# Visit tables, GAT weight preparation and first node stage as one block of a two-layer graph network kernel

## The reference, cut to what matters

```
h = relu(layernorm(x))                      # x: 6250 x 256
x = x + layer0(h, src, dst)                 # GAT attention (4 heads), then q/k attention
h = relu(layernorm(x))
x = x + layer1(h, src, dst, edge_type, edge_weight)   # typed GAT (8 heads), layernorm, FFN
# GAT of layer 0, the first that reads the node table:
hw = h @ gat_W;  a_src, a_dst = sums of hw * att_src, hw * att_dst per head
alpha = segment_softmax(leaky_relu(a_src[src] + a_dst[dst]), dst)
x1 = segment_sum(hw[src] * alpha, dst)
```

## Time and profile before

| | |
|---|---|
| median of 3 runs | 4923.0 us (4912.32 to 4923.89) |
| profiled execution, its own time | 4959.05 us |
| its span, first to last instruction | 4957.4 us |
| mean granted TensorE clock | 0.788 |
| busy in the span | PE 67%, DVE 65%, POOL 59%, ACT 46% |
| DMA | 118 GB/s mean |

### The profile page before, as it was taken

One profiled execution on the slowest core, in us unless ns is written; L12 is line 12 of the kernel. 1 busy time (PEld: TensorE's weight loads), 2 busy tenths in 40 slices (PEclk: granted clock), 3 DMA queues, 4 the chain that ended last, 5 costly groups with the idle time before them and its releaser, 6 DMA issues. The chain is left out here.

```text
span 4957.4 us, 74006 instructions
## 1 busy us (share of the span) xinstructions
PE 3333.3 (67%) x13766; PEld 2197.6 (44%) x13766; DVE 3239.2 (65%) x11427; ACT 2269.2 (46%) x6293; POOL 2911.1 (59%) x3158
## 2 busy tenths in 40 slices
PE   0536666766676657777777777836667666765998
PEld 0424444434443434444444444523444444434887
DVE  4546666666667946665656566847777777776665
ACT  0224555555553335555555555525545545553332
POOL 1266666666662456666666662366666666661776
PEclk9956766576668978898888889967676676677999
DMA  5345444544442334444434433544444444441221
GB/s 54 107 133 146 143 141 140 149 140 141 141 143 67 115 101 113 112 114 113 112 113 117 114 113 103 190 135 132 130 133 133 135 132 130 133 131 55 63 68 49
DMA packets 313472, 586.81 MB, mean 118 GB/s; under 512 B 106395, under 2 KB 204231, under 8 KB 313111
## 3 DMA queue, kind: packets, MB, share of 16 engines
q0 software_dynamic: 122944, 354.78, 26.1%
q1 hardware_dynamic: 147832, 188.48, 13.3%
q10 hardware_dynamic: 42336, 39.66, 2.3%
HBM read 504.91 MB, written 77.73 MB: 118 GB/s over the span
## 5 line engine op out<-in xcount | busy, mean ns | idle before, releaser
L561 PE MATMUL psum<-big,onehot 128*128 128x264 f32 (+2 forms) x4992 | 2149.5, 547 | 842.1 <-DVE big L733 312.8
L561 PEld LDWEIGHTS psum<-big,onehot 128*128 128x128 f32 x4992 | 1063.4, 253 | 1225.0 <-issue 675.2
L755 DVE TENSOR_TENSOR acc<-acc,psum 128x264 f32 (+2 forms) x2496 | 1051.3, 421 | 595.2 <-PE psum L561 372.0
L446 POOL DMA_INDIRECT big<-table_attn,tables x832 | 787.7, 947 | 499.8 <-PE psum L561 189.2
L446 POOL DMA_INDIRECT big<-table_gat,tables x832 | 841.1, 1011 | 403.8 <-issue 205.2
L446 POOL DMA_INDIRECT big<-table_typed,tables x832 | 816.7, 982 | 429.5 <-issue 215.3
L472 ACT ACTIVATE dist<-iota,tables 128x128 f32<-128x128 f32 x2496 | 1000.0, 401 | 101.2 <-DMA tables<-edge_tables 14.3
L484 ACT ACTIVATE onehot<-dist,ones 128x128 f32<-128x128 f32 x1664 | 649.6, 391 | 854.1 <-PE psum L561 552.5
L518 PE MATMUL psum<-big,onehot_t 128*128 x2496 | 484.6, 308 | 239.0 <-issue 144.7
L597 DVE CUSTOM_DVE_ANT_0 junk<-psum,big 128x258 f32<-128x258 f32 x832 | 344.6, 415 | 323.7 <-DMA joins<-visit_joins 174.4
L481 ACT ACTIVATE onehot<-dist,weight,neg_weight 128x128 f32<-128x128 f32 x832 | 400.4, 482 | 318.9 <-PE psum L561 184.4
(11 more groups left out here) (251 smaller groups left out, 3625.9 us busy)
## 6 DMA issues: line engine op xcount, KB each, us to landing
onehot_t<-onehots SPq DMA_DIRECT2D x104, 512.0 KB
big<-visit_positions SPq DMA_DIRECT2D x52, 512.0 KB
onehots<-onehot_t SPq DMA_DIRECT2D x52, 512.0 KB
seg<-visit_segments SPq DMA_DIRECT2D x676, 24.1 KB
big<-table_gat,tables POOLq DMA_INDIRECT x832
big<-table_attn,tables POOLq DMA_INDIRECT x832
big<-table_typed,tables POOLq DMA_INDIRECT x832
big<-in_x_dram SPq DMA_DIRECT2D x98, 128.0 KB
```

The source lines that it names most:

```text
L446: pool.indirect_dma_start(X[:, v % RING, :], None, ph.table, bass.IndirectOffsetOnAxis(ap=column(k, 0)[:, g:g + 1].bitcast(I32), axis=0)). ...
L561: nc.tensor.matmul(sum_ps(v), m.onehot[:, v % 4, :], X[:, v % RING, 0:ph.WS], start=True, stop=True).then_inc(S["summed"], 1)
L755: nc.vector.tensor_tensor(row, row, sum_ps(v), ALU.add).then_inc(S["added"], 1)
```

## The change

`visits`, `prepare_gat` and `nodes_in` become one block, `visits_and_nodes_in`, without barriers within. The order on each engine is written out: an iterator `step` over 54 node steps is drawn from between the links of the visit chain. Two node steps stand ahead of the counting, one in each further round of it, two behind it; then four in each chunk; six between the last chunk and the joins; ten behind them. The loops over blocks are unrolled, with constants in the waits. The functions of a node block stay as they were, but for one lag more on PE and ACT (`project` of i-2, `turn` of i-1).

Besides the order, five things change:

- All seven chunks have record buffers of their own (in `acc`), and the gathers of chunk c+2 are issued when chunk c begins.
- A chunk's DVE work is shorter: one conversion of 128 x 512 for four of 128 x 128, one operation less for `rel`, one copy less for `scal`. Three of six packing copies go to ACT as one instruction (`pack_rest`).
- The joins are computed on 56 partitions (a batch each) with 16 to 64 columns, not on one partition with up to 3584. They are stored in two transfers instead of eight.
- `blocks` is read from memory as integers. `cont` and `first_hot` are spread over the partitions by one matmul with `ones`, not through memory.
- SP's one queue holds the loads of x, the stores of the chunks and the reads for the joins, in the order of the code.

```diff
-def nodes_in(nc, m, args, dram, w, sp_):
+def visits_and_nodes_in(nc, m, args, dram):
+    v_, n_ = Space(m.acc), Space(m.big[:, 0:16384])
+    rec = [v_.take(4 * P).bitcast(I32) for _ in range(VC)]
+    wrec = [v_.take(P) for _ in range(VC)]
+    before = [v_.take(NV // 2).bitcast(BF16) for _ in range(2)]
+    fields, rel, last_f, in_block, tmp, dst_s = v_.take(4, P), *(v_.take(P) for _ in range(5))
...
+    STEPS = NB + 5
...
+            for c in range(VC):
+                for _ in range(2):
+                    load(next(step))
+                sp.wait_ge(S["chunk"], c + 1)
+                sp.dma_start(dram.scal[:, c * P:(c + 1) * P].rearrange("a v -> v a"), scal[c % 2], allow_slow_non_contiguous=True).then_inc(S[f"stored{c % 2}"], 16)
+                sp.dma_start(dram.rel16[c * P * P:(c + 1) * P * P].rearrange("(v e) -> v e", e=P), rel16[c % 2]).then_inc(S[f"stored{c % 2}"], 16)
+                sp.dma_start(dram.segs[c * P:(c + 1) * P, 1:SEG], seg[c % 2][:, 1:SEG]).then_inc(S[f"stored{c % 2}"], 16)
+                for _ in range(2):
+                sp.wait_ge(S["packed"], c + 1)
+                sp.wait_ge(S["packed_rest"], c + 1)
+                sp.dma_start(dram.tables[c * (P // G):(c + 1) * (P // G), :, :].rearrange("k p a -> p k a"),
+                             packed[c % 2].rearrange("p (k a) -> p k a", a=A * G)).then_inc(S[f"tables{c % 2}"], 16)
+            sp.wait_ge(S["stored0"], (VC - VC // 2) * 48)
+            sp.wait_ge(S["stored1"], VC // 2 * 48)
+            sp.dma_start(rows, dram.scal[0:3, :].rearrange("a (k g) -> k a g", g=G)).then_inc(S["rows"], 16)
+            sp.dma_start(prev[0:1, 1:G], dram.scal[1:2, 0:G - 1]).then_inc(S["rows"], 16)
+            sp.dma_start(m.blocks[:, :], dram.scal[3:4, :].bitcast(I32)).then_inc(S["end"], 16)
+            for b in step:
+                load(b)
+            sp.wait_ge(S["outs"], 1)
+            for twice in range(2):
+                sp.dma_start(dram.joins[:, :, twice, :], outs).then_inc(S["end"], 16)
+            sp.dma_start(dram.segs[:, 0:1].rearrange("(k g) a -> k (g a)", g=G), bias0, allow_slow_non_contiguous=True).then_inc(S["end"], 16)
...
+            def records(c):
+                pool.indirect_dma_start(rec[c], None, dram.edges, bass.IndirectOffsetOnAxis(ap=tile_i[:, c:c + 1], axis=0)).then_inc(S[f"rec{c}"], 16)
+                pool.indirect_dma_start(wrec[c], None, dram.weights, bass.IndirectOffsetOnAxis(ap=tile_i[:, c:c + 1], axis=0)).then_inc(S[f"wrec{c}"], 16)
+            for _ in range(8):
+                rstd(next(step))
+            pool.wait_ge(S["tiles"], 1)
+            records(0)
+            rstd(next(step))
+            records(1)
+            rstd(next(step))
+            for c in range(VC):
+                if c + 2 < VC:
+                    records(c + 2)
+                for _ in range(4):
+                    rstd(next(step))
+            for b in step:
+                rstd(b)
...
+            def node(i):
+                store(i - 3)
+                copy_row(i - 2)
+                relu(i - 1)
+
+            def pack_rest(c):
+                act.wait_ge(S["turned_chunk"], c + 1)
+                if c >= 2:
+                    act.wait_ge(S[f"tables{c % 2}"], c // 2 * 16)
+                whole = packed[c % 2].rearrange("p (k a g) -> p a k g", a=A, g=G)
+                nc.scalar.activation(whole[:, 3:6, :, :], ps[:, 5 + 2 * (c % 2), 0:3 * P].rearrange("p (a k g) -> p a k g", a=3, g=G), ACT.Copy).then_inc(S["packed_rest"], 1)
+            step = iter(range(STEPS))
+            for _ in range(10):
+                node(next(step))
+            for c in range(VC):
+                for _ in range(4):
+                    node(next(step))
+                pack_rest(c)
+            for i in step:
+                node(i)
...
+            def node(i):
+                project(i - 2)
+                turn(i - 1)
+
+            def count(c):
+                pe.wait_ge(S["before"], c + 1)
+                for q in range(VC):
+                    last = nc.tensor.matmul(counts[:, c * VC + q:c * VC + q + 1], before[c % 2][:, q * P:(q + 1) * P], one16[:, 0:1], start=True, stop=True)
+                last.then_inc(S["counted"], 1)
+
+            def turn_chunk(c):
+                pe.wait_ge(S["chunk"], c + 1)
+                pe.wait_ge(S[f"wrec{c}"], 16)
+                if c == 0:
+                    pe.wait_ge(S["summed"], 1)
+                if c >= 2:
+                    pe.wait_ge(S["packed"], c - 1)
+                    pe.wait_ge(S["packed_rest"], c - 1)
+                for i, a in enumerate([src_f, rel, last_f, et_f, wrec[c]]):
+                    last = nc.tensor.transpose(turned_at(c, i), a, m.ident[:, :])
+                last.then_inc(S["turned_chunk"], 1)
+            for _ in range(2):
+                node(next(step))
+            for c in range(VC):
+                count(c)
+                if c == 1:
...
+                    last.then_inc(S["logit_w"], 1)
+                if c:
+                    node(next(step))
+            for _ in range(2):
+                node(next(step))
+            for c in range(VC):
+                for _ in range(3):
+                    node(next(step))
+                turn_chunk(c)
+                node(next(step))
+            for i in step:
+                node(i)
+            pe.wait_ge(S["outs"], 1)
+            pe.wait_ge(S["packed"], VC)
+            nc.tensor.matmul(ps[:, 4, 0:2 * KB], m.ones[0:KB, :], diag.rearrange("p a k -> p (a k)"), start=True, stop=True).then_inc(S["firsts"], 1)
...
+            def node(i):
+                own_logits(i - 5)
+                normalize(i - 1)
+                stats(i)
...
+            for _ in range(2):
+                node(next(step))
+            dve.wait_ge(S["last_dst"], 16 * sum(c * P < NT for c in range(VC)))
+            for c in range(VC):
+                if c >= 2:
+                    dve.wait_ge(S["counted"], c - 1)
+                nc.vector.tensor_scalar(before[c % 2], v_row, v_end[:, c:c + 1], None, ALU.is_gt).then_inc(S["before"], 1)
+                    dve.wait_ge(S["w_turned"], 1)
+                    nc.vector.tensor_copy(turned_w, ps[:, 5:7, 0:D]).then_inc(S["masked"], 1)
+                    nc.vector.tensor_copy(w[:, :, 0:D], raw)
+                if c == 2:
+                if c:
+                    node(next(step))
+            dve.wait_ge(S["counted"], VC)
+            c_.step(nc.vector.tensor_copy(t_idx, counts[:, 0:VC]))
...
+            nc.vector.tensor_copy(tile_i, t_idx).then_inc(S["tiles"], 1)
+            for _ in range(2):
+                node(next(step))
+            for c in range(VC):
+                p = c % 2
+                dve.wait_ge(S[f"rec{c}"], 16)
+                if c:
+                    dve.wait_ge(S["turned_chunk"], c)
+                if c > 1:
+                    dve.wait_ge(S[f"stored{p}"], c // 2 * 48)
+                c_.step(nc.vector.tensor_copy(fields.rearrange("p a e -> p (a e)"), rec[c]))
...
+                c_.step(nc.vector.tensor_scalar(in_block, tmp, 0.0, None, ALU.is_ge))
+                node(next(step))
+                c_.step(nc.vector.scalar_tensor_tensor(in_block, tmp, float(P - 1), in_block, ALU.is_le, ALU.mult))
...
+                c_.step(nc.vector.tensor_scalar(rel, rel, FAR, None, ALU.add))
...
+                nc.vector.tensor_copy(rel16[p], rel)
+                nc.vector.tensor_copy(scal[p][:, 2:3], rel[:, 0:1]).then_inc(S["chunk"], 1)
+                for _ in range(3):
+                    node(next(step))
+                dve.wait_ge(S["turned_chunk"], c + 1)
...
+                src_t, rel_t = (turned_at(c, i).rearrange("p (k g) -> p k g", g=G) for i in range(2))
+                nc.vector.tensor_copy(ints[:, :, 0, :], src_t)
+                nc.vector.tensor_scalar(whole[:, :, 2, :], rel_t, FAR / 2, -BIG, ALU.is_gt, ALU.mult)
+                nc.vector.tensor_copy(whole[:, :, 1, :], rel_t).then_inc(S["packed"], 1)
+            for _ in range(6):
+                node(next(step))
+
+            dve.wait_ge(S["rows"], 48)
...
+            nc.vector.tensor_scalar(diag[:, 1, :], m.ident[0:KB, 0:KB], rel0[:, 0:1], None, ALU.mult)
+            nc.vector.tensor_scalar(outs, outs, -1.0, BIG, ALU.add, ALU.mult).then_inc(S["outs"], 1)
+            for i in step:
+                node(i)
+            split3(c_, nc, lambda s: tab[:, :, s, :], m.self_logit[:, :, H0:2 * H0], rest)
+            dve.wait_ge(S["firsts"], 1)
+            nc.vector.tensor_copy(m.cont[:, :], ps[:, 4, 0:NBATCH])
+            c_.step(nc.vector.tensor_scalar(m.first_hot[:, :], ps[:, 4, KB:KB + NBATCH], m.pcol[:, 0:1], None, ALU.is_equal))
...
-        visits(nc, m, dram)
-        space = Space(m.arena)
-        w = prepare_gat(nc, m, args, space)
-        nodes_in(nc, m, args, dram, w, space)
+        visits_and_nodes_in(nc, m, args, dram)
```

(25 more changed lines are left out.)

421 lines of the change are left out of this document (151 added, 270 removed).

## The result

The changed kernel took 4832.0 us (median of 4 runs, 4829.7 to 4834.9), the kernel before 4922.2 us beside it (4912.3 to 4923.9). The ratio is 0.9826, with a 95% interval from 0.9811 to 0.9840. That is 90 us less by the medians and 86 us (79 to 93) by the ratio; it was forecast to be 92. The forecast time was 4831.

A forecast was written before the change was run, and what follows sets the result against it. No engine was full before the edge pass: three stages ran one behind the other, the visits as one chain. Opening to 38.1, seven chunks to 122.1 and tail to 158.7 gained 92.4 us, scaled 91.7: 4831, range 4810 to 4850.

The forecast's parts named there:

- Opening: Loads, weight preparation and counting: first `project` at 18.3 us, tile numbers at 33.6, first chunk at 38.1.
- 16 us later: In the opening, tile numbers would exist at 33.6 us, against 17.25 in the kernel before.
- A chunk: One visit chunk with four node steps: 12.0 us, taken between 10.6 and 13.2; seven chunks 84 us.
- DMA wants: In the chunks, transfers of visits and node blocks together need 13.2 us a chunk, if the earlier busy share adds up.
- The floor of 10.6: DVE's work in a chunk with four node steps, 10.6 us, leading PE and ACT's 9.8 if loads are in time.
- The wait priced at nothing on SP: The x load behind three chunk stores goes out 1.4 us late, covered by three steps; uncovered, 10 us in all.
- loads late: Rival: once a chunk an x load or row store needs 10 us more; 39 us more, 4870; chance 0.17.
- The wait on POOL: In the chunks, the next 1/sqrt stands behind two gathers (2.5 us), covered by DVE's work; uncovered, 17 us in all.
- PE at the lower level: Rival: PE stays at 3.02 us a step in the merged block; 32 us more, 4863; chance 0.15.
- Tail: Behind the chunks: twelve steps at 2.0 us, joins 1.9, last block normalized at 148.0, edge pass starting at 158.7.
- swallowed: Rival: the block is faster, but the other 4706 us, equal by code, run otherwise; chance 0.05.
- slower rival: Rival: x loads land so late that the edge pass starts past 251.1 us, from landings of 14.0 us; chance 0.03.

The follow-up runs named there:

- chain_first: `quads_x8_r8` with the ten node steps of the opening moved into the chunks (six in each of the first three, five in the others); ratio 0.9798.
- quads: The changed kernel with the visit scalars stored as 128 pieces of 16 bytes a chunk instead of 512 scattered pieces of 4 bytes; 4809.2 us, ratio 0.9784.
- quads_segs2: The changed kernel with 16-byte stores of the scalars and the segment masks' store made twice (192 KB more a chunk); 4806.9 us, ratio 0.9777.
- scal2: The changed kernel with the scattered store of the scalars made twice, the second into a tensor nothing reads; 4875.4 us, ratio 0.9920.
- serial: The changed kernel with no node step in the opening or the chunks, and gathers of chunk c+2 waiting for chunk c-1; 4853.2 us, ratio 0.9875.
- quads_x8_r8: The changed kernel with 16-byte stores of the scalars and eight x and eight row buffers in place of four; 4802.1 us, ratio 0.9774.
- warm: `quads_x8_r8` with 28 useless transposes on PE ahead of the weights; ratio 0.9781.

## Why the prediction was right, and where its steps were not

The forecast was right in its path: the same chain, in the same order, with most terms within 1.3 us. The sum, term by term, by the trace of the changed kernel:

| term | predicted | measured |
|---|---|---|
| first `project` | 18.3 | 17.1 |
| tile numbers | 33.6 | 32.6 |
| first chunk starts | 38.1 | 38.5 |
| seven chunks | 84.0 | 88.1 |
| joins | 1.9 | 1.4 |
| last packing to last block normalized | 25.9 | 27.2 |
| from there to the edge pass | 10.8 | 7.1 |
| edge pass starts | 158.7 | 161.0 |

That 4831 met 4832.0 within 1 us is luck. The chunks were 4.1 us too cheap and the end 3.7 too dear, and the gain by the ratio, 86 us, is 6 below the one forecast.

- **Opening.** Right in size. I had two steps at the lower level and three at 2.0 us; it was four and one between (17.06 to 29.14). The 1.2 us by which the weights were sooner, and counts that hid beside these slow steps, made up for it. That this part is "16 us later" was right and, by `chain_first`, no loss.
- **A chunk.** 12.6 against 12.0, but the reasoning behind 12.0 failed. The 13.2 us that "DMA wants" took the share of 0.88 in the earlier trace rows as a price that adds up. It was mostly waiting behind the scattered store: `quads` moves the same bytes in chunks of 10.0 us, and `quads_segs2` more bytes in 9.9. The floor of 10.6 was a little too high as well. I had taken the middle of two numbers, and the truth lay there for a third reason: that this term came out near was luck. The rule quoted from the Trainium skill (DMA: Bandwidth & Descriptors, section "Issuing engines are not separate DMA queues"), that the queues share 16 engines, agrees with the trace in that the loads of SP, the stores of ACT and the gathers of POOL were all held up. A pace of 13.2 us did not follow from it.
- **The wait priced at nothing on SP.** The cover of three steps did not hold. DVE waited 17.3 us for x in the chunks and 5.9 behind them, the rival *loads late* in a mild form. The 1.4 us of issue were not the cause: with 16-byte stores the same order on SP leaves no wait for x in the chunks and one of 3.4 us behind them. The wait on POOL was seen once, as 1.40 us at 36.09, and in the chunks 14 waits make 8.2 us, none over 0.6: it cost nothing.
- **PE at the lower level.** Partly there. Some groups in the chunks take 2.1 us, and the granted clock reads 0.75 there. Up to the edge pass 15 of the 49 groups take over 1.9 us. `quads` has 10 such groups, and 0.88 in its chunks. PE's slow groups stretch its busy time from 50.7 us (`quads`) to 58.4 and 64.0 (`scal2`). How much of the 12.6 us is theirs was not separated from the held-up loads.
- **Tail.** Steps behind the chunks went at 1.82 us where x was there (DVE's own pace), not 2.0; the stall of 5.35 us took this back. From the last normalized block the rest took 3.7 us less than forecast. Against the earlier trace rows it is 2.8 us less. Four blocks' own logits were left to copy in both; in the changed kernel the first two waited for nothing, in the kernel before each waited 1.5 to 1.7 us for ACT. That PE and ACT had caught up during the stall is the likely reason; no run tests it.
- **"What would show it".** Edge pass near 159: 161. Last-chunk store near 120: 125 (its L775 store at 124.98). DVE idle before normalize near 0.5 in two of four steps: 0.6, 14 times. Tile numbers near 34: 32.6. Joins under 2.5: 1.4. Gathers never waited for: one wait of 1.17 us at the first chunk. From one conversion to the next 10.6 to 13.2: from 10.1 to 15.0, three of the six outside. Of the signs of being wrong two were there, in small: groups of 2.1 us in the chunks, and DVE waiting for x and ACT for row stores. The forecast was right in spite of them.
- **What the forecast did not divide.** It summed an absolute order and never asked what the node steps in the opening and the chunks add by themselves. `serial` did: about a third of the gain, 31 of 90 us by the traces, 24 of 86 by the ratios. The larger part came from shorter work, fewer barriers and waits that now run beside other work, which no run divides further.
- **The rivals' prices.** The prediction says that its range, up to 4868, takes in *loads late*; that rival was priced at 4870, just outside. The result does not depend on it.
- **Not slower, not swallowed.** DVE never waited longer than 5.4 us for a load of x, and the median landings, 7.2 us for row stores and 9.9 for record gathers, stayed below the 14 us of the slower rival. Only doubling the store (`scal2`, 14.3 us for row stores) reached it, and even that kernel stayed 0.8% below the kernel before. Almost all of the gain in the edge pass's start, 90.1 us, is in the times (86 to 90, with an interval from 79 to 93), so little or nothing was swallowed.

## What to carry to other kernels

Read a DMA share beside its GB/s. A full share at a third of the rate reached elsewhere is a queue held up, and the smallest transfer can be the cause: look at how it is cut and where its pieces go, not only at its bytes. When a merge does several things, build a kernel that has only some of them; here the one without node steps in the opening and the chunks had two thirds of the gain. To say that overlap is worth only the last third would need a kernel without the other overlap, too. And more buffers (14 us) bridge a block that the removal of its cause (21 us) makes unnecessary.

## What the hardware showed that I had not expected

- 512 scattered pieces of 4 bytes, 2 KB in all, held up transfers on SP's, ACT's and POOL's queues. In the chunks, from `quads` to the changed kernel is 2.6 us a chunk (18.0 / 7), and from there to `scal2` 4.8 us (33.6 / 7): the second store costs more than the first. That buffers bridge a part of the first only would explain it. As 128 pieces of 16 bytes the same data cost nothing that could be seen.
- Which property of that store does it is open: `quads` changes the size of the pieces, their number and their addresses at once. Pieces of 4 bytes alone are not enough. Behind the joins (148.85 us) SP stores one column of the segment masks as 896 pieces of 4 bytes, 1540 bytes apart, and the row stores around it land in 2.2 us, by the issue rows of the changed kernel from 148 to 162 us. Two things differ there: the pieces have no close neighbours in HBM, and the queues carry less, 65 GB/s. The chunk loop of the kernel before was held up at 79 GB/s, which speaks for the addresses, but no run parts the two.

```profile
table_gat<-big ACTq DMA_DIRECT2D x6, 132.0 KB, 2.2
...
visit_segments<-big SPq DMA_DIRECT2D x1, 3.5 KB
```

- 192 KB more a chunk cost nothing that shows beside 16-byte stores. Beside scattered ones they cost 11 us by the trace, which the times do not show (0.9833 against 0.9826).
- The number of slow `project` groups at the start differs between executions with the same work ahead of them: five and one between in `quads_x8_r8`, four and one in the changed kernel, one and one in `quads`. From 17 to 33 us the granted clock reads 1.00 in all three, and 0.77 in `warm`, which had fewer slow groups than the first two. In so short a stretch the reading does not count them.
